# The first key's q k products of four-key tiles move from VectorE to GpSimd

## What is computed

```python
xn  = (x - mean(x)) / sqrt(var(x) + 1e-5)
q, k, v = split(xn @ Wqkv.T + bqkv, 3)            # 16 heads of 32
scores  = mask + 32**-0.5 * einsum('bnd,bmd->bnm', q, k)
# mask: positions 0 to 3 see keys 0 to 3 only; positions 4 to 7 see all 8 keys
out = x + (softmax(scores) @ v) @ Wproj.T + bproj + (fp8(xn) as f16) @ fp8(Wffn).T + bffn
```

## Time and profile before

| | us |
|---|---|
| median of three runs | 1539.74 |
| profiled execution, its own time | 1538.02 |
| span of the profile | 1536.2 |
| PE busy | 1492.5 (97%) |
| VectorE busy | 1463.5 (95%) |
| GpSimd busy | 1320.6 (86%) |
| ScalarE busy | 1271.9 (83%) |

### The profile page before, as it was taken

One profiled execution on the slowest core, in us unless ns is written; L12 is line 12 of the kernel. 1 busy time (PEld: TensorE's weight loads), 2 busy tenths in 40 slices (PEclk: granted clock), 3 DMA queues, 4 the chain that ended last, 5 costly groups with the idle time before them and its releaser, 6 DMA issues.

```text
span 1536.2 us, 24273 instructions
## 1 busy us (share of the span) xinstructions
PE 1492.5 (97%) x6872; PEld 676.3 (44%) x6872; DVE 1463.5 (95%) x1220; ACT 1271.9 (83%) x3019; POOL 1320.6 (86%) x1035
## 2 busy tenths in 40 slices
PE   6999999999999999999999999999999999999966
PEld 3444444444444444444444444444444444444422
DVE  6999999999999999999999999999999999999897
ACT  5679889797988979788797988979788897988754
POOL 2578998999898899989998998899989988998885
PEclk9999999999999999999999999999999999999988
DMA  7444554545555554544545455554645555454333
GB/s 225 89 102 103 132 123 119 128 115 130 115 131 119 118 131 108 131 122 112 133 116 120 115 127 123 116 126 114 135 109 118 135 112 132 118 120 113 87 85 101
DMA packets 368694, 184.61 MB, mean 120 GB/s; under 512 B 316336, under 2 KB 316336, under 8 KB 368560
## 3 DMA queue, kind: packets, MB, share of 16 engines
q1 hardware_dynamic: 368560, 183.06, 50.5%
HBM read 73.41 MB, written 33.55 MB: 70 GB/s over the span
## 4 chain that ended last, share of the span: by engine, by line
PE 84%; DVE 4%; issue 3%; POOL 2%; ACT 0%; DMA 0%; SPq 0%; DVEq 0%; POOLq 0%; ACTq 0%
PE proj_ps L723 19%; PE k_ps L723 19%; PE q_ps L723 19%; PE v_ps L723 19%; PE lin_ps L742 6%; PE proj_ps L772 2%; DVE prod_qk L882 1%; DVE o_nat L998 1%; POOL prod_pv L466 1%; DVE scores L887 1%; ACT prod_pv L569 0%; POOL xs L525 0%; DMA xT<-x 0%; DMA oT<-o 0%; ACT o L624 0%
## 5 line engine op out<-in xcount | busy, mean ns | idle before, releaser
L466 POOL TENSOR_TENSOR prod_pv<-kv,probs 128x2048 f32<-128x2048 f32 x192 | 645.8, 3364 | 9.9
L998 DVE TENSOR_REDUCE o_nat<-prod_pv 128x512 f32<-128x2048 f32 (+1 forms) x128 | 429.1, 3352 | 31.7 <-ACT prod_pv L569 19.2
L887 DVE TENSOR_REDUCE scores<-prod_qk 128x64 f32<-128x2048 f32 x192 | 439.3, 2288 | 6.8 <-DVE prod_qk L882 0.2
L882 DVE TENSOR_TENSOR prod_qk<-q_ps,kv 128x1536 f32<-128x1536 f32 (+1 forms) x192 | 398.0, 2073 | 0.2 <-issue 0.2
L723 PE MATMUL k_ps<-wqkv_hi,xT 128*128 128x512 f16 x1024 | 326.0, 380 | 1.6 <-DMA xT<-x 1.4
L723 PE MATMUL v_ps<-wqkv_hi,xT 128*128 128x512 f16 x1024 | 325.5, 379 | 0.0
L723 PE MATMUL q_ps<-wqkv_hi,xT 128*128 128x512 f16 x1024 | 325.5, 379 | 0.0
L723 PE MATMUL proj_ps<-wproj_hi,oT 128*128 128x512 f16 x1008 | 324.3, 383 | 0.0
L569 ACT ACTIVATE prod_pv<-kv,probs 128x32 f32<-128x32 f32 x1024 | 260.3, 341 | 0.0
L673 ACT ACTIVATE kv<-v_ps 128x512 f32<-128x512 f32 x128 | 140.8, 1100 | 86.4 <-PE v_ps L723 86.4
L723 PE MATMUL k_ps<-wqkv_lo,xT 128*128 128x512 f16 x512 | 194.6, 380 | 0.0
(11 more groups left out here) (118 smaller groups left out, 1954.7 us busy)
## 6 DMA issues: line engine op xcount, KB each, us to landing
xn<-in_L_attn_x SPq DMA_DIRECT2D x128, 256.0 KB, 2.8
xs<-in_L_attn_x SPq DMA_DIRECT2D x128, 256.0 KB, 2.6
out<-xs SPq DMA_DIRECT2D x128, 256.0 KB, 2.1
xT<-x SPq DMA_TRANSPOSE x256, 3.0
kv<-in_L_attn_Wqkv SPq DMA_DIRECT2D x3, 1024.0 KB, 8.1
oT<-o SPq DMA_TRANSPOSE x128, 3.2
kv<-in_L_attn_Wproj SPq DMA_DIRECT2D x1, 1024.0 KB, 5.9
prod_pv<-in_L_ffn_weight SPq DMA_DIRECT2D x1, 1024.0 KB, 9.7
```

Source lines behind the costliest of these rows:

```text
L466: nc.gpsimd.tensor_tensor(o, v, p, ALU.mult).then_inc(pv_multiplied, 1)
L882: nc.vector.tensor_tensor(prod_qk[:, 1:1 + m0 + 4 - m1, :], qb, k, ALU.mult).then_inc(qk_multiplied, 1)
L887: nc.vector.tensor_reduce(scores[:, n % 2, :, m0:m0 + 4].rearrange("p h m -> p m h"), prod_qk[:, row:row + 4, :].rearrange("p m (h d) -> p ...
L998: nc.vector.tensor_reduce(o_nat[:, n % 2, :], prod_pv[:, place:place + units, :].rearrange("p q (c m) -> p c q m", m=4), AX_XY, ALU.add).t ...
```

## The change

GpSimd now makes the first key's q k product for four-key tiles too. ScalarE copies the query for them as well, and VectorE's product for such a tile has three keys and not four. The counts of the semaphores go by all tiles instead of the eight-key ones. The reduction keeps its four rows.

```diff
@@ GpSimd, slot
-                if live(i, j, L_FIRST) and keys_of(j - L_FIRST) == N:
+                if live(i, j, L_FIRST):
                     n = j - L_FIRST
-                    after(pool, q_copied, heavy_count(i, n))
+                    after(pool, q_copied, tile_count(i, n))
                     after(pool, k_kept, tile_count(i, N * (n // N)))
                     after(pool, qk_reduced, unit_count(i, units_before(n - 1)))
                     nc.gpsimd.tensor_tensor(prod_qk[:, 0, :], q_first[:, :], k_all[:, (n // N) % 2, 0, :],
@@ ScalarE, slot
-                if live(i, j, L_FIRST) and keys_of(j - L_FIRST) == N:
+                if live(i, j, L_FIRST):
                     n = j - L_FIRST
                     after(act, q_summed, tile_count(i, n))
-                    after(act, first_key_multiplied, heavy_count(i, n - 1))
+                    after(act, first_key_multiplied, tile_count(i, n - 1))
                     nc.scalar.activation(q_first[:, :], q_ps[n % 4][:, :], ACT.Copy).then_inc(q_copied, 1)
@@ VectorE, scores_of_unit
-                shared = keys_of(n) == N and m0 == 0
+                shared = m0 == 0
                 row, m1 = (0, m0 + 1) if shared else (1, m0)
...
                 if shared:
-                    after(dve, first_key_multiplied, heavy_count(i, n))
+                    after(dve, first_key_multiplied, tile_count(i, n))
```

## The result

The changed kernel takes 1556.41 us, the median of 4 runs (1555.45 to 1557.41), against 1539.65 (1538.12 to 1540.12, 4 runs) in the same measurement: a ratio of 1.0111 [1.0093, 1.0128], 16.8 us slower. 1555 was forecast. The profiled execution took 1557.41, its span is 1555.6.

A forecast was written before the change was run, and what follows sets the result against it. PE bounded the steady stretch; a new ring of 92.28 us a group would decide. 14 rings plus 33.47 gave 1325.39 against 1309.01, net 15.4 on 1538.02, 1553.4; with 1.7 to the median 1555 us, range 1541 to 1566.

The forecast's parts named there:

- "faster" rival: VectorE's relief counts at the start and the drain, PE starting 1.6 to 2 us earlier: 1537; chance 0.05.
- The new wait: GpSimd's product for tile 57 may start only when tile 56's reduction is over; tile 54's probs are queued behind it.
- ring: Loop of waits through VectorE and GpSimd, A + B + C = 92.28 us a group against PE's 91.51, setting the pace.
- rival "no change": PE's cover holds and VectorE gains slack; needs B at 24.31 or less: 1540 to 1541; chance 0.14.
- B: GpSimd from the end of tile 56's first-unit reduction to VectorE's sum over keys of tile 55: 25.08 us.
- A: VectorE from the end of tile 51's first-unit reduction to that of tile 56: 59.33 less 0.52, 58.81 us.
- C: VectorE from tile 55's sum over keys to the end of tile 59's first-unit reduction: 8.91 less 0.52, 8.39 us.
- way through B: GpSimd's products, or ScalarE's copy and last key, up to VectorE's sum: 24.82 against 24.80 us, neither hiding the other.
- The rival in which the two trade delays: GpSimd's and ScalarE's ways release each other in three slots: 0.3 to 1.0 us a group, 1559 to 1569; chance 0.15.
- S(8): Time when the reduction of tile 8's first unit is over: 142.62 before, forecast 0.5 earlier through its shorter product.
- the four early tiles' products: 0, within 1: At the start, the four early tiles' products stand in slots where GpSimd still waits: 0 us, within 1.
- S(123): End of tile 123's first-unit reduction, where the last light tiles end: 1451.63 before, forecast net 15.4 us later.

The follow-up runs named there:

- first tile alone: Changed kernel, but of the four-key tiles GpSimd takes only each group's first; against the kernel before: 1539.06 us, ratio 0.9999.
- second alone: Changed kernel, but of the four-key tiles GpSimd takes only each group's second, 16 of 64 products; against the kernel before: 1553.82 us, ratio 1.0097.
- fourth alone: Changed kernel, but of the four-key tiles GpSimd takes only each group's fourth; against the kernel before: 1539.98 us, ratio 1.0004.
- all but the second: Changed kernel, but GpSimd takes each group's first, third and fourth four-key tile, not the second; against the kernel before: 1539.75 us, ratio 1.0009.
- copies alone: ScalarE makes all 128 query copies, GpSimd and VectorE work as in the kernel before; against that kernel: 1539.21 us, ratio 1.0005.
- VectorE's saving alone: VectorE's four-key tiles take three keys, nobody makes the first key's product or added copy; against the kernel before: 1538.33 us, ratio 0.9991.
- all the work, the wait moved: Changed kernel, but second and fourth four-key tiles use the fourth key in row 4, waiting one tile further back; against the kernel before: 1539.83 us, ratio 1.0011.
- four products again: Changed kernel, but VectorE makes all four products again, still waiting for GpSimd's, which is thrown away; against the kernel before: 1572.14 us, ratio 1.0218.

## Why the prediction was right, and where a size was off

**What bounds the kernel.** PE did, before the change. That VectorE's relief is worth next to nothing at PE's pace is shown by the run with that relief alone: -0.1%, 1.0 to 1.1 us, where the prediction's "faster" rival put it at over 2.

**The new wait closes a ring that decides.** Shown from both sides: with the one product of the second four-key tile the loss is there, with all but that one 1.3 to 1.5 us are left of 17.5, and with all the work but without that wait 1.7. The rival "no change" needed B at 24.31 or less; B is 25.18.

**A, B and C.** A was forecast at 58.81 and is 58.80; C at 8.39 and is 8.39; B at 25.08 and is 25.18. Of B's terms the hand-over from GpSimd to VectorE, of which no row told, was taken as 0.2 and is 722.52 - 722.23 = 0.29. The ring is 92.37 to 92.40 instead of 92.28, over 14 turns 1.7 us.

**Neither way through B hides the other.** This held, and stayed harmless. On ScalarE's timeline the copies wait for GpSimd in each of the slots, and the sum over keys is released by GpSimd:
```profile
698.95 0.60 ACT L605 ACTIVATE q_first<-q_ps 128x512 f32<-128x512 f32 x1 [1.24 <-POOL prod_qk L519]
...
711.25 0.60 ACT L605 ACTIVATE q_first<-q_ps 128x512 f32<-128x512 f32 x1 [0.31 <-POOL prod_qk L519]
...
720.12 2.04 ACT L569 ACTIVATE prod_pv<-kv,probs 128x32 f32<-128x32 f32 x8
722.05 1.09 ACT L673 ACTIVATE kv<-v_ps 128x512 f32<-128x512 f32 x1
```
ScalarE's last key is done at 722.16 (720.12 + 2.04), GpSimd's products at 722.23, so the two ways still end together. The rival in which the two trade delays, 0.3 to 1.0 us a group on top, would show more than the hand-over's 0.1 over the sum: it fell.

**The start: -0.5 was wrong, it is +0.4.** S(8) stands at 143.00 and not at 142.62 - 0.52. The step "the four early tiles' products: 0, within 1" is the one mis-sized, by 0.9. Between 50 and 145 us VectorE waits 3.0 us for loads of x where it waited 1.7, the longest of them at 72.33, and once for the new product:
```profile
72.33 0.69 DVE L972 BATCH_NORM_STATS2 stats<-xn 128x6 f32<-128x512 f32 x1 [2.51 <-DMA xn<-in_L_attn_x]
...
81.11 2.29 DVE L887 TENSOR_REDUCE scores<-prod_qk 128x64 f32<-128x2048 f32 x1 [0.37 <-POOL prod_qk L519]
```
The other kernels have S(8) at 142.03 (first tile alone), 142.60 (second alone), 143.19 (fourth alone), 142.49 (all but the second), 142.94 (copies alone), 142.35 (VectorE's saving alone) and 142.31 (all the work, the wait moved). So products and copies do delay the start, the fourth tile's by 0.6; all of VectorE's saving by itself brings 0.3 there and not 0.5; and 0.7 of the 0.9 is gone when the waits are moved. These shifts don't add up, each is from one profile, and which of them makes the 0.9 stays open. (The prediction's 4.3 for the lag at the start is 142.62 - 138.38 = 4.24; nothing hangs on it.)

**The sum.** Forecast: +15.4 to S(123) and to the end. Measured: +17.8 to S(123), made up of 0.9 at the start, 1.7 in the rings and -0.2 in the last B and C (32.80 against 33.47 - 0.5 = 32.97) beside the 15.4. Behind S(123) nothing was to change, and within a level nothing did: 84.60 before the change, 84.62 with the second tile alone and with four products again. Medians say +16.8; they mix two levels of the end, and within a level the difference is 17.4 or 17.5 (1538.12 to the mean of 1555.45 and 1555.61; 1539.81, the mean of the other three runs, to that of 1557.21 and 1557.41). So the forecast was short by 2 us and not by the 1.4 that 1555 against 1556.41 shows. The 1.7 that it added from the profiled run to the median is about the distance of the two levels, and the median of two lower and two upper runs fell between them: that much of the nearness is luck.

**The page's factor.** The prediction weighed the Trainium skill's "GPSIMD Engine Reference", section "Engine selection". The trace after agrees with the direction and gives the larger ratio: 1.23 us of GpSimd's time (697.59 to 698.82) for the 0.52 that VectorE saved, a factor of 2.4.

## What to carry to other kernels

When an instruction is added to an engine that has idle time, look at what it waits for and what is queued behind it, and add up the loop that the wait closes: here 92.3 us against a pace of 91.5, which no busy share shows. A ring is priced from the trace before the change: on each engine take the time from the moment it is released to the moment it releases the next one, and add these up. Where a ring decides, try a wait for an older user of the buffer: here another row took away nine tenths of the loss with all the work still there. Even then the move can be worth nothing, as here, so leave the work out altogether first to see what its removal could bring.

## What the runs showed of the hardware

**A stretch at the lower clock lies on the last projection or doesn't.** The 27 runs of the kernel before in the second comparison lie at 1537.95 to 1538.27 (13 of them) and at 1539.35 to 1539.98 (14), with none between. Every kernel here has two such levels, about 1.6 us apart (those with the ring have few runs: 1555.45 and 1555.61, 1557.21 and 1557.41 for the changed one). The difference arises behind S(123): from there to the end of the span are 84.60 to 84.63 in six profiles and 86.17 to 86.31 in the four others. By stretch, in the kernel before (profiled at 1538.02):
```profile
1505.00:1512.00 7.00, 7.00 (x27) 2.85 (x25) 5.63 (x3) 6.66 (x25) 7.00 (x3) 0.76 0.41 114
...
1522.00:1527.00 5.00, 2.44 (x9) 1.06 (x10) 4.30 (x3) 1.11 (x2) 0.00 (x0) 0.87 0.45 119
1527.00:1530.00 3.00, 2.24 (x7) 0.51 (x5) 1.10 (x2) 0.69 (x1) 0.00 (x0) 0.64 0.69 175
1530.00:1533.00 3.00, 2.92 (x13) 1.13 (x13) 0.04 (x1) 0.00 (x0) 0.00 (x0) 1.00 0.23 87
```
and in the changed one (1557.41):
```profile
1540.00:1545.00 5.00, 2.48 (x12) 1.19 (x13) 4.30 (x3) 1.11 (x2) 0.00 (x0) 1.00 0.50 142
1545.00:1548.00 3.00, 0.75 (x4) 0.13 (x3) 0.89 (x2) 0.69 (x1) 0.00 (x0) 0.92 0.78 207
1548.00:1551.00 3.00, 3.00 (x8) 1.06 (x7) 0.00 (x0) 0.00 (x0) 0.00 (x0) 0.51 0.14 55
```
The clock falls more than once behind S(123): in the kernel before the granted clock is 0.76 from 1505 to 1512, back at 1.00 from 1512 to 1522, and then 0.87 and 0.64 in the next two stretches, with PE busy for 2.44 of 5 and 2.24 of 3 us. In the changed kernel a stretch at the lower level (granted 0.51 over 3 us, that is 1.2 GHz) lies on the last projection; PE had been busy for 0.75 of the 3 us ahead of it. In the kernel before, the stretch lies ahead of the last projection, which runs at 1.00. In all ten profiles of this case a last projection with matmuls of 0.63 us goes with a time of the upper level (four), and one at 0.38 throughout with the lower level (six). Seven or eight of its twelve matmuls at 0.43 apart instead of 0.22 make about the 1.6 us, an estimate from these rows. What puts the stretch there in one execution and not in another stays open. So of two kernels whose medians differ by 1.6 us one may only have met the other level more often.

**The hand-overs.** From VectorE's reduction, as S(56) reads it, to GpSimd's next instruction 0.25 us (697.34 to 697.59), from the end of GpSimd's products to VectorE's sum 0.29 (722.23 to 722.52). Either is a third of the 0.8 us on which the ring decided.
